# Linear attention brought into the wide attention's block, with its numerators ahead of the projection and its division ahead of the addition

## The chip, the cores and the metric

The kernel runs on one NeuronCore of a Trainium2 chip. The metric is the device time of one execution in microseconds (us); lower is better. The core's engines run separate instruction streams: TensorE (matmuls and transposes; in the profile PE, and PEld for its weight loads), VectorE (DVE), ScalarE (ACT), GpSimd (POOL) and SyncE (SP, which only issues DMAs here). They are ordered against each other by semaphores: an instruction waits until a counter has reached a value, and counts another one up when it is done.

## The reference, cut to what matters

A batch of 16 sequences of 128 tokens with 256 features goes through two decoder layers, each with an attention, a cross step over a context `ctx` and a feed-forward step; every step is added to `x`. The change lies in the second layer, where the wide attention (16 heads of 128) is followed by a linear attention over `ctx` and by a mixture of experts:

```python
q = heads(layernorm(x) @ Wq.T + bq)       # 16 heads of 16
k = heads(ctx @ Wk.T + bk); v = heads(ctx @ Wv.T + bv)
q_prime = relu(q @ Wqf.T)                  # 64 features a head
k_prime = relu(k @ Wkf.T) * mask
kv  = einsum('bhnf,bhne->bhfe', k_prime, v)
num = einsum('bhmf,bhfe->bhme', q_prime, kv)
den = einsum('bhmf,bhf->bhm', q_prime, k_prime.sum(2))
x = x + (num / (den + 1e-8)) @ Wo.T + bo
```

## The kernel before, in words

`kernel` runs two stages. The first holds all of layer one and the wide attention. The second, `stage_linear_attention_and_expert_mix` (L2480), holds linear attention and the expert mixture. Between them every engine drains, the block ends with a barrier of all engines, GpSimd clears the semaphores and a second barrier follows (`release_semaphores`, L59 to L63).

**Products.** `product` (L39) multiplies two float32 matrices, each split into a rounded high part and a rest, by three matmuls of type fp32r: high by high, high by low, low by high (L41, L42, L43). Operands for it are split by a copy on ScalarE and a subtraction on VectorE. A plain float32 matmul shows as two TensorE records.

**Wide attention, last group.** Its four groups of four sequences each run 16 heads (`group`). Per head t, TensorE does the scores of the next head (L1072), the q and k projections of the one after, the output projection of the former head, the transposes of the probabilities (L1113), values for a later head, and the weighing of values (`weigh`, L1123). VectorE masks, takes the row maximum, copies k (L1488) and the transposed probabilities (L1536), and makes the low part of the weighed values (L1549) after ScalarE has made the high one (L1330). In the last group the heads 14 and 15 have no projections ahead of them. After head 15, VectorE adds four banks to `x` (L1561).

**Linear attention** (`linear_attention`) works by batches (sequences) n = 0 to 15, four to a quarter g; j is the place in the quarter. Its prologue, before the loop: load `ctx` for the first quarter and then for the rest, load five small tensors, split the four weights into high and low, normalise x of the second quarter, and on TensorE three products to fill the time (L1898), queries and keys of quarter 0, query features (L1801), key features (L1812), values, and `key_values(0)`.

The loop, in TensorE's order, for each n: `key_features(n+1)` (L1812), `project(n-1)` (in the last batch after the next one), `numerators_and_denominators(n)` (L1835), then, by j, query features of the next quarter (L1801, j = 2, 3), queries (j = 1, 2) and keys (j = 0, 1; for quarter 1 also n = 2), transposes of the normalised x (L164), `values(n+2)`, and `key_values(n+1)` (L1822). From n = 12 on, transposes for the expert mixture take the place of those of the next quarter.

`key_values` makes kv for two heads at once: 8 matmuls with 128 columns of `kp` as weights and 64 columns of `va` moving. Of the four blocks of each product only the two of one head with itself are used. `numerators_and_denominators` has 16 matmuls, each with 32 columns of weights, on the four strips of 32 columns of the array in turn. `project` reads `oT`, the high and low part of the output of the division.

ScalarE, for each n: the denominators plus 1e-8 (`den`, L1974), query features, queries and keys, the high part of the divided output (`keep_o`, L1979), and kv into SBUF (L1968). It also makes the high part of ctx for the next quarter (L1945).

VectorE, for each n: key features with relu and mask (L2044), `update(n-1)`, that is adding the projection to x (L2063), `divide(n)`, a reciprocal (L2050) and a multiplication (L2052), values (L2038), the low part of the divided output (`o_rest`, L2057), low parts of x and of ctx (L175, L2030), and statistics of x (L112 to L119) or its normalisation (L152). At n = 3 it also sets up the expert mixture (L2237 to L2244).

Waits that bind the loop: `key_values(n+1)` writes the bank that `project(n-1)` wrote, so it waits until `update(n-1)` has read it; `numerators_and_denominators(n+1)` waits until `divide(n)` has read its bank; both use kv from ScalarE.

Of the kernel before, what the change touches and what calls it, by code (L numbers as in the profile page):

```python
# [11 lines left out]
P = 128  # L12
# [10 lines left out]

class Chain:


    def __init__(self, eng, sem, it, per):
        self.eng, self.sem, self.it, self.per, self.n = eng, sem, it, per, 0

    def done(self, ins):  # L30
        self.n += 1
        ins.then_inc(self.sem, 1)
        self.eng.wait_ge(self.sem, self.it * self.per + self.n)
# [16 lines left out]
class Program:  # L50
    def __init__(self, nc, io):
        self.nc, self.io = nc, io
        self.sems = []

# [137 lines left out]
def lora_attention(pr, ctx):  # L192
# [55 lines left out]
    lora_loaded = sem("lora_loaded")  # L248
    NLOAD = 6

# [543 lines left out]
def stage_attention_conv_experts_and_wide_attention(pr, lora):  # L794
# [10 lines left out]
    with ExitStack() as ctx:  # L805
        sb = lambda n, shape, dt=F32: ctx.enter_context(nc.sbuf_tensor(f"wa_{n}", shape, dt))
# [33 lines left out]
        w_in = [sem(f"weights_loaded{n}") for n in range(4 * H // VH)]  # L840
# [13 lines left out]
        u_ps, u_ok = sem("lora_in_psum"), sem("lora_added")  # L854
        block = ctx.enter_context(nc.Block())
# [47 lines left out]
        def _(sp):  # L903
            lora_sync(sp)

            def load_piece(hb, m):
                sp.dma_start(pr.wide_raw[hb][:, m], io["wide_w"][hb, :, m]).then_inc(w_in[PIECES.index((hb, m))], 16)
# [15 lines left out]
            sp.dma_start(pr.h_or_w[:], io["li_w"]).then_inc(pr.w_loaded, 16)  # L923

        @block.gpsimd
        def _(pool):
# [14 lines left out]
            def group(it, last):  # L941
                for t in range(H):
# [4 lines left out]
                    if in_range(t + 1, last):  # L947
                        normalise(it * H + t + 1, (t + 1) % 2)

# [15 lines left out]
            for it in range(NG):  # L965
                group(it, it == NG - 1)

        @block.tensor
        def _(pe):
# [169 lines left out]
            def group(it, last):  # L1139
                n_v = G  # L1140
                for t in range(H):
# [22 lines left out]
                    if t == T_TURN:  # L1164
# [3 lines left out]
                        norm.tensor_transpose(pe, next_norm(it))  # L1168
                    weigh(it, t)
                    for unit in late:  # L1170
# [68 lines left out]
            for it in range(NG):  # L1239
                group(it, it == NG - 1)  # L1240

        @block.scalar
        def _(act):
# [17 lines left out]
            def high_part(n):  # L1261
                hb, m = PIECES[n]
                act.wait_ge(w_in[n], 16)
# [49 lines left out]
            def group(it, last):  # L1313
                for t in range(H):
# [69 lines left out]
            for it in range(NG):  # L1384
                group(it, it == NG - 1)

        @block.vector
        def _(dve):
# [135 lines left out]
            def group(it, last):  # L1524
# [3 lines left out]
                for t in range(H):  # L1528
# [26 lines left out]
                    if it == 0 and 1 <= t <= len(PIECES) - FRONT_PIECES:  # L1555
                        low_part(FRONT_PIECES + t - 1)
                    if t == H - 1 and not last:
# [69 lines left out]
            for it in range(NG):  # L1627
                group(it, it == NG - 1)


def first_layer_and_wide_attention(pr):
# [3 lines left out]
    with ExitStack() as ctx:  # L1635
# [29 lines left out]
        stage_attention_conv_experts_and_wide_attention(pr, lora)  # L1665


def linear_attention(pr, ctx, mix):

    nc, io, x, banks = pr.nc, pr.io, pr.x, pr.banks
# [948 lines left out]
```

## Time and profile before

| | |
|---|---|
| time, median of 3 runs | 1010.68 us (1008.8 to 1012.94) |
| the profiled execution's own time | 1011.92 us |
| its span, first to last instruction | 1010.1 us |
| TensorE busy | 959.6 us, 95% of the span |
| VectorE busy | 636.9 us, 63% |
| ScalarE busy | 482.0 us, 48% |
| GpSimd busy | 239.3 us, 24% |
| mean granted TensorE clock | 0.98 of full speed |

Busy time says how much of the span an engine had an instruction in work. The granted clock is a share of 2.4 GHz; the rows show either 1.0 or 0.5 of it (1.2 GHz). The chain of waits is followed back from the last instruction, each step to what released it; a chain row gives its start, its length, and the engine, tile and line. A timeline row gives the start, the length, the engine, the line and the operation, and in brackets how long the engine idled before it and what ended that.

### The profile page before, as it was taken

The numbers are of one execution on the slowest core, as the hardware profiler recorded it, in microseconds if no ns is written. First come the engines' busy times: TensorE is split into PE (matmuls) and PEld (weight loads), VectorE is DVE, ScalarE is ACT, GpSimd is POOL, SyncE is SP. The second block draws the span as 40 slices with busy tenths as digits, with TensorE's granted clock in tenths as the row PEclk, the third lists the DMA queues.
The fourth block names the chain that finished last, engine by engine and source line by source line (L and its number), as shares of the span: only waits on it lengthen the run. The fifth ranks groups of instructions, "written<-read, shape, count | busy, mean of one in ns | idle before, by whom it ended". The sixth has DMA issues, their size and how long they took to land. (4 is left out here: it accounts for less than half of the span.)

```text
span 1010.1 us, 19622 instructions
## 1 busy us (share of the span) xinstructions
PE 959.6 (95%) x7403; PEld 820.1 (81%) x7403; DVE 636.9 (63%) x1399; ACT 482.0 (48%) x1611; POOL 239.3 (24%) x257
## 2 busy tenths in 40 slices
PE   7999999999999999999999999999999888999877
PEld 5777777898788888888888888888888757777757
DVE  5678887897765666544554645464554555777854
ACT  3887877334455454353434534444444343344421
POOL 3455786760011111111111111111111130110000
PEclk9999999999999999999999999999999997899979
DMA  8000000003400000000000000000000070000002
GB/s 303 27 2 2 2 2 1 2 15 133 177 14 1 1 1 1 2 1 1 1 1 1 1 1 16 28 1 1 1 2 1 1 268 1 2 1 2 2 1 84
DMA packets 10395, 27.85 MB, mean 28 GB/s; under 512 B 1792, under 2 KB 6944, under 8 KB 9664
## 3 DMA queue, kind: packets, MB, share of 16 engines
q1 hardware_dynamic: 9584, 26.41, 7.2%
q8 instruction: 60, 0.98, 0.4%
q10 hardware_dynamic: 720, 0.20, 0.1%
q14 instruction: 31, 0.25, 0.1%
HBM read 24.51 MB, written 2.10 MB: 26 GB/s over the span
## 5 line engine op out<-in xcount | busy, mean ns | idle before, releaser
L938 POOL TENSOR_TENSOR wa_prob<-wa_prob,wa_rsum 128x512 f32<-128x512 f32 x64 | 67.5, 1055 | 412.5 <-DVE wa_rsum L1493 412.5
L1296 ACT ACTIVATE wa_prob<-wa_prob,wa_negmax 128x128 f32<-128x128 f32 x256 | 99.8, 391 | 56.8 <-DVE wa_negmax L1482 56.6
L41 PE MATMUL bank<-norm_xT_hi,wide_hi 128*128 128x512 f32 x256 | 106.0, 414 | 0.2 <-DVE norm_xT_lo L175 0.2
L42 PE MATMUL bank<-norm_xT_lo,wide_hi 128*128 128x512 f32 x256 | 101.0, 395 | 0.0
L43 PE MATMUL bank<-norm_xT_hi,wide_lo 128*128 128x512 f32 x256 | 101.0, 395 | 0.0
L1549 DVE TENSOR_TENSOR wa_z_lo<-bank,wa_z_hi 128x512 fp32r<-128x512 f32 x64 | 44.3, 691 | 86.6 <-ACT wa_z_hi L1330 86.2
L562 ACT ACTIVATE v_prob<-bank,la_negmax 128x128 f32<-128x128 f32 x256 | 91.1, 399 | 1.1 <-DVE la_negmax L640 1.1
L1304 ACT COPY wa_q<-bank 128x512 f32<-128x512 f32 x64 | 37.5, 586 | 99.0 <-PE bank L43 99.0
L1311 ACT COPY wa_v<-bank 128x512 f32<-128x512 f32 x64 | 37.3, 585 | 97.1 <-PE bank L43 97.1
L308 POOL TENSOR_TENSOR v_prob<-v_prob,la_rsum 128x512 f32<-128x512 f32 x64 | 66.5, 1041 | 52.5 <-DVE la_rsum L645 52.4
L41 PE MATMUL bank<-wide_hi,wa_z_hi 128*128 128x256 f32 x256 | 73.6, 287 | 1.7 <-DVE wa_z_lo L1549 1.4
L159 POOL TENSOR_TENSOR norm_rstd<-norm_rstd,minus_half 128x4 f32<-128x4 f32 x23 | 24.8, 1079 | 205.4 <-DVE norm_rstd L119 174.4
L1123 PEld LDWEIGHTS bank<-wa_probT,wa_v 128*128 128x128 f32 x512 | 65.4, 191 | 9.7 <-DVE wa_probT L1536 4.0
L1488 DVE COPY wa_k<-bank 128x512 f32<-128x512 f32 x64 | 44.3, 692 | 45.2 <-PE bank L43 44.9
L43 PE MATMUL bank<-wide_hi,wa_z_lo 128*128 128x256 f32 x256 | 72.4, 283 | 0.0
L42 PE MATMUL bank<-wide_lo,wa_z_hi 128*128 128x256 f32 x256 | 72.3, 282 | 0.0
L1123 PE MATMUL bank<-wa_probT,wa_v 128*128 128x128 f32 x512 | 68.2, 276 | 1.9 <-DVE wa_probT L1536 1.9
L1536 DVE COPY wa_probT<-bank 128x512 f32<-128x512 f32 x64 | 44.0, 688 | 40.7 <-PE bank L1113 40.7
L1072 PE MATMUL bank<-wa_k,wa_q 128*128 128x128 f32 x512 | 67.6, 275 | 0.0
L1072 PEld LDWEIGHTS bank<-wa_k,wa_q 128*128 128x128 f32 x512 | 62.7, 192 | 0.4
L562 ACT ACTIVATION_READ_ACCUMULATOR v_prob<-bank,la_negmax 128x1 f32 x256 | 61.0, 238 | 0.0
L43 PEld LDWEIGHTS bank<-norm_xT_hi,wide_lo 128*128 128x128 f32 x256 | 48.0, 187 | 11.8
(282 smaller groups left out, 2462.8 us busy)
## 6 DMA issues: line engine op xcount, KB each, us to landing
wide_raw<-in_wide_w SPq DMA_DIRECT2D x16, 512.0 KB, 6.4
em_w<-in_em_w SPq DMA_DIRECT2D x1, 4096.0 KB, 16.1
x<-in_x SPq DMA_DIRECT2D x4, 512.0 KB, 4.8
lc_kt<-in_ctx_rev SPq DMA_DIRECT2D x1, 2048.0 KB, 10.6
lc_toep<-in_toeplitz SPq DMA_DIRECT2D x1, 2048.0 KB, 14.5
out_x<-x SPq DMA_DIRECT2D x8, 256.0 KB, 2.9
li_kt<-in_ctx_rev SPq DMA_DIRECT2D x1, 1536.0 KB, 8.2
w_or_y<-in_l_w SPq DMA_DIRECT2D x1, 1024.0 KB, 6.5
```

The source lines that it names most:

```text
L41: nc.tensor.matmul(out, a[0], b[0], start=start, stop=False, skip_group_check=True)
L42: nc.tensor.matmul(out, a[0], b[1], start=False, stop=False, skip_group_check=True)
L43: return nc.tensor.matmul(out, a[1], b[0], start=False, stop=stop, skip_group_check=True)
L308: nc.gpsimd.tensor_tensor(own, own, rsum[:, n % NS, :].unsqueeze(2).to_broadcast([P, 4, P]), ALU.mult)\
L562: last = nc.scalar.activation(prob[:, n % NP, s, :], b_s[n % RG][:, s * P:(s + 1) * P], ACT.Exp, bias=negmax[:, n % NS, s:s + 1], accum_ou ...
L938: nc.gpsimd.tensor_tensor(prob[:, s], prob[:, s], rsum[:, s, :].unsqueeze(2).to_broadcast([P, G, P]), ALU.mult).then_inc(prob_ok, 1)
L1072: last = nc.tensor.matmul(b_s[s][:, t], q[:, s, t], k[:, s, t], start=True, stop=True)
L1123: last = nc.tensor.matmul(b_z[:, j * P:(j + 1) * P], v[:, g % 2, j, m * HD:(m + 1) * HD], probT[:, h_ % 2, j, :], start=True, stop=True)
L1296: last = nc.scalar.activation(prob[:, s, j, :], prob[:, s, j, :], ACT.Exp, bias=negmax[:, s, j:j + 1], scale=SCALE, accum_out=sums[:, s, j ...
L1488: nc.vector.tensor_copy(k[:, s, :], b_p[1][:, :]).then_inc(k_ok, 1)
L1536: nc.vector.tensor_copy(probT[:, t % 2], b_t[:, :].rearrange("p (j k) -> p j k", j=G))\
L1549: nc.vector.tensor_tensor(z[1][:, t % 2, :], b_z[:, :], z[0][:, t % 2, :].bitcast(F32), ALU.subtract).then_inc(z_lo, 1)
```

## The change

The two stages become one, `both_layers`. The barrier pair and the clearing of semaphores between them go; the events of linear attention and of the mixture reuse semaphores of layer one that nothing waits on any more, each with a base (`Event`, `reached`). The buffers of linear attention lie where those of the layer one attention and convolution and the first half of the wide weights were.

The prologue moves into the last group of the wide attention, at fixed heads t. The products that filled time go. Loads of ctx are issued when head 3 is projected. The split of ctx is done once for all four quarters, ahead of the loop. `project` becomes a plain float32 product. `key_values` becomes 16 matmuls of 64 columns of weights and 32 moving columns, two heads of a pair on the two halves of the array's columns. On TensorE `numerators_and_denominators(n)` goes ahead of `project(n-1)`; on VectorE `divide(n)` ahead of `update(n-1)`. The set-up of the mixture moves to n = 1 and n = 5, and the transposes of its similarity matrix from behind the loop into n = 14. The high part of a wide weight now waits for all four loads of its quarter.

```diff
+Event = namedtuple("Event", "sem base")
+def reached(eng, event, count):
+    eng.wait_ge(event.sem, event.base + count)
...
-            sp.dma_start(pr.wide_raw[hb][:, m], io["wide_w"][hb, :, m]).then_inc(w_in[PIECES.index((hb, m))], 16)
+            sp.dma_start(pr.wide_raw[hb][:, m], io["wide_w"][hb, :, m]).then_inc(w_in[hb], 16)
...
-            act.wait_ge(w_in[n], 16)
+            act.wait_ge(w_in[hb], 16 * 4)
...
+                    if last and t == H - 1:
+                        linear.tensor_keys(pe, 0)
                     weigh(it, t)
+                    if last:
+                        linear.tensor_early(pe, t)
+                        norm.enter_stage(2, 1, b_p)
+                    if last and t == H - 1:
+                        linear.tensor_keys(pe, 1)
...
+                    if last:
+                        linear.scalar_early(act, t)        # after z_hi
...
+                    if last:
+                        linear.vector_early(dve, t)        # after z_lo and low_part
```

In `linear_attention`:

```diff
+    KT_AT, W_AT = 6, 10
+    QUERIES_AT, KEYS_AT = 14, 15
+    STATS_AT, CLEAR_AT, APPLY_AT = 7, 10, 14
...
+    def tensor_early(pe, t):
+        if t == QUERIES_AT:
+            pe.wait_ge(norm.s_lo, DC * norm.split(0))
+            reached(pe, w_lo, 3)
+            for m in range(DC):
+                queries(pe, 0, m, banks[m])
+    def tensor_keys(pe, m):
+        reached(pe, qT_ok, m + 1)
+        keys(pe, 0, m, banks[m])
...
+    def scalar_early(act, t):
+        if KT_AT <= t < KT_AT + NG:
+            reached(act, kt_in, 16 * NG)
+            nc.scalar.copy(kt[0][:, :, own], kt32[:, :, own]).then_inc(kt_hi.sem, 1)
+        if W_AT <= t < W_AT + 3:
+            nc.scalar.copy(w[0][:, n], w32[:, n]).then_inc(w_hi.sem, 1)
+        if t == QUERIES_AT:
+            for m in range(DC):
+                keep_qT(act, 0, m, banks[m])
+        if t == KEYS_AT:
+            for m in range(DC):
+                keep_kT(act, 0, m, banks[m])
+    def vector_early(dve, t):
+        if KT_AT <= t < KT_AT + NG:
+            nc.vector.tensor_tensor(kt[1][:, :, own], kt32[:, :, own], kt[0][:, :, own].bitcast(F32), ALU.subtract)
+        if W_AT <= t < W_AT + 3:
+            nc.vector.tensor_tensor(w[1][:, n], w32[:, n], w[0][:, n].bitcast(F32), ALU.subtract)
+        if t in (STATS_AT, APPLY_AT):
+            if t == STATS_AT:
+                norm.vector_stats(dve, 1)
+            else:
+                norm.vector_apply(dve, 1)
...
             for t in range(T):
-                last = nc.tensor.matmul(b_kv[:, t * 2 * VW:(t + 1) * 2 * VW], kp[:, n % 2, t, :],
-                                        va[:, n % 2, 2 * t:2 * t + 2, :], start=True, stop=True)
+                for e in range(2):
+                    last = nc.tensor.matmul(b_kv[F * e:F * e + F, t * VW:(t + 1) * VW],
+                                            kp[:, n % 2, t, F * e:F * e + F], va[:, n % 2, 2 * t + e, :],
+                                            start=True, stop=True)
...
         def project(n):
-            pe.wait_ge(ot_lo, n + 1)
+            reached(pe, o_ok, n + 1)
...
-                last = product(nc, b_kv[:, 0:D], pair(oT, slice(None), n % 2, c), pair(w, slice(None), O, c),
-                               c == 0, c == DC - 1)
+                last = nc.tensor.matmul(b_kv[:, 0:D], o[:, n % 2, c, :], w32[:, O, c, :], start=(c == 0),
+                                        stop=(c == DC - 1))
...
         reached(pe, loaded, 16 * NLOAD)
         query_features(0, 0)
+        first_query_features()          # waits for kT_ok and for the wide attention's last x
         key_features(0)
+        reached(pe, qf_first, 1)
         values(0)
+        turn_x(1, 0)
         key_values(0)
         values(1)
         for n in range(NB):
...
-            if 0 < n < NB - 1:
-                project(n - 1)
             numerators_and_denominators(n)
-            if n == NB - 1:
+            if n > 0:
                 project(n - 1)
...
-            keep_o(n)
...
+            divide(n, chain)
             if n > 0:
                 update(n - 1)
-            divide(n, chain)
...
-            o_rest(n)
...
-            if t + 1 < NG and j == 3:
-                kt_rest(t + 1)
-            if n == 3:
+            if n == SETUP_AT:
                 mix.vector_setup(dve)
+            if n == LENGTH_AT:
+                mix.vector_length(dve)
```

## Rows read from the trace of the kernel before

**Rows 1.** Windows: stretch, its length, busy time (instructions) of each engine, PEclk, DMA.
```profile
836.80:847.00 10.20, 10.20 (x77) 8.76 (x76) 3.84 (x5) 1.79 (x4) 0.00 (x0) 0.51 0.00 0
877.40:884.20 6.80, 6.80 (x64) 5.66 (x64) 4.11 (x8) 1.99 (x5) 0.00 (x0) 0.50 0.00 0
```

**Rows 2.** Chain of waits in the loop: start, length, what.
```profile
837.08 3.31 PE bank L1822 x16
859.91 1.73 PE bank L1822 x16
...
902.85 1.73 PE bank L1822 x16
...
905.46 0.36 PE bank L41
905.82 0.12 PE bank L42
...
907.85 0.23 PE bank L42
...
910.45 1.73 PE bank L1822 x16
927.02 1.73 PE bank L1822 x16
933.56 1.73 PE bank L1822 x16
940.61 1.73 PE bank L1822 x16
```

**Rows 3.** Timeline, TensorE in batch 10, at full clock.
```profile
926.85 1.89 PE L1822 MATMUL bank<-li_va,li_kp 128*128 128x64 f32 x16
928.68 0.73 PE L1812 MATMUL bank<-li_wf,li_kT 32*128 32x128 f32 x16
930.51 1.08 PE L1835 MATMUL bank<-li_qp,li_kv 128*32 128x128 f32 x32
```

**Rows 4.** Timeline, the loop's last batches.
```profile
935.45 1.40 DVE L112 BATCH_NORM_STATS2 norm_stats<-x 128x6 f32<-128x256 f32 x4
937.38 1.28 DVE L2044 TENSOR_SCALAR li_kp<-bank,li_mask 128x1024 f32<-128x1024 f32 x1
...
952.31 0.47 ACT L1974 ACTIVATE li_den<-bank,li_tiny 128x256 f32<-128x256 f32 x1 [0.97 <-PE bank L1835]
952.81 1.97 PE L1822 MATMUL bank<-li_va,li_kp 128*128 128x64 f32 x16 [0.57 <-DVE x L2063]
952.82 1.75 DVE L2050 RECIPROCAL li_rden<-li_den 128x256 f32<-128x256 f32 x1 [0.15 <-ACT li_den L1974]
955.37 0.74 ACT L1968 COPY li_kv<-bank 64x256 f32<-64x256 f32 x2
959.71 0.42 DVE L2063 TENSOR_TENSOR x<-bank,x 128x256 f32<-128x256 f32 x1 [2.16 <-PE bank L43]
964.96 0.42 DVE L2063 TENSOR_TENSOR x<-bank,x 128x256 f32<-128x256 f32 x1 [0.92 <-PE bank L43]
```

**Rows 5.** Timeline, TensorE around the stage boundary.
```profile
800.15 1.16 PE L1123 MATMUL bank<-wa_probT,wa_v 128*128 128x128 f32 x8 [0.43 <-DVE wa_probT L1536]
806.94 0.39 PE L41 MATMUL bank<-wide_hi,wa_z_hi 128*128 128x256 f32 x1 [1.40 <-DVE wa_z_lo L1549]
811.62 0.67 PE L1898 MATMUL bank<-h_or_w 128*128 128x512 f32 x1 [2.99 <-PEq L62]
```

**Rows 6.** Timeline, VectorE in the last group's head 8, and one low part of ctx.
```profile
755.19 0.69 DVE L1488 COPY wa_k<-bank 128x512 f32<-128x512 f32 x1 [0.86 <-PE bank L43]
757.06 0.69 DVE L1536 COPY wa_probT<-bank 128x512 f32<-128x512 f32 x1 [1.18 <-PE bank L1113]
...
869.11 1.22 DVE L2030 TENSOR_TENSOR li_kt_lo<-li_kt,li_kt_hi 128x1024 fp32r<-128x1024 f32 x1
```

**Rows 7.** Timeline, plain float32 products with 256 moving columns.
```profile
259.70 1.96 PE L1006 MATMUL bank<-le_u,xe 128*128 128x256 f32 x8
```

More of the change, by code:

```diff
@@ L1 @@
+from collections import namedtuple
 from contextlib import ExitStack
@@ L248, in lora_attention @@
     lora_loaded = sem("lora_loaded")
+    pr.finished += [Event(q_ps, DC * NG), Event(q_ok, DC * NG), Event(k_ps, DC * NG), Event(k_ok, DC * NG),
+                    Event(v_ps, 2 * NG), Event(v_ok, 2 * NG), Event(s_ps, N), Event(max_ok, N), Event(exp_ok, N),
+                    Event(r_ok, N), Event(prob_ok, N), Event(t_ps, N), Event(t_ok, N), Event(av_ps, N),
+                    Event(ot_hi, NB), Event(ot_lo, NB), Event(o_ps, NB), Event(x_ok, NB), Event(xb_ok, NB),
+                    Event(kk_first, 4 * CONV_C), Event(c_ps, CONV_H), Event(c_ok, CONV_H), Event(w_ps, 4),
+                    Event(w_f32, 4), Event(w_hi, 4), Event(w_lo, 4), Event(bias_ps, 1), Event(bias_ok, 1),
+                    Event(qb_ok, 1), Event(v_zero, 1), Event(loaded, 16 * 6), Event(lora_loaded, 16 * 2)]
     NLOAD = 6
@@ L805, in stage_attention_conv_experts_and_wide_attention @@
     with ExitStack() as ctx:
-        sb = lambda n, shape, dt=F32: ctx.enter_context(nc.sbuf_tensor(f"wa_{n}", shape, dt))
+        sb = lambda n, shape, dt=F32: layer.enter_context(nc.sbuf_tensor(f"wa_{n}", shape, dt))
         sem = lambda n: pr.sem(f"wa_{n}")
@@ L839, in stage_attention_conv_experts_and_wide_attention @@
         loaded = sem("masks_loaded")
-        w_in = [sem(f"weights_loaded{n}") for n in range(4 * H // VH)]
+        w_in = [sem(f"weights_loaded{n}") for n in range(H // VH)]
         w_hi, w_ok = sem("weights_hi"), sem("weights_ready")
@@ L854, in stage_attention_conv_experts_and_wide_attention @@
         u_ps, u_ok = sem("lora_in_psum"), sem("lora_added")
+        pr.wide_o_ps, pr.wide_u_ps, pr.wide_x_ok = o_ps, u_ps, x_ok
+        pr.finished += [Event(kk_ok, 4), Event(sq_ok, 2), Event(c_ps, 3 * CH), Event(c_ok, 3 * CH),
+                        Event(yq_ok, NG * C), Event(slot_ps, NG * C), Event(cx_ok, NG * G), Event(new_ps, G),
+                        Event(nbias_ok, 1)]
+        layer.close()
+        mix = ExpertMix(pr)
+        linear = linear_attention(pr, lambda n, shape, dt=F32: ctx.enter_context(nc.sbuf_tensor(n, shape, dt)), mix)
+        mix.allocate(ctx)
         block = ctx.enter_context(nc.Block())
@@ L1556, in group @@
                         low_part(FRONT_PIECES + t - 1)
+                    if last:
+                        linear.vector_early(dve, t)
                     if t == H - 1 and not last:
```

1494 lines of the change are left out of this document (747 added, 747 removed).

## The prediction

> **What bounds the kernel now.** The profile was read in this order: the page, the chain of waits from its end backwards, windows over the stages, and the timeline on both sides of the stage boundary. Three stretches matter.
>
> The first is the boundary. `weigh` of head 14 ends at 800.15 + 1.16 = 801.3. The last projection starts at 806.9 after 1.40 us of waiting for the low part, x is then added, and the second stage's first product starts at 811.6, after 2.99 us in which TensorE waited for the barrier [rows 5]. From there to `key_values(1)` at 837.1 [rows 2] comes the prologue, where TensorE waits for splits, copies and the loaded context. So 801.3 to 837.1 is 35.8 us.
>
> The second is the loop. At full clock its chain is TensorE's own work: the starts of `key_values` are 7.6 us apart for j = 0 (902.85 to 910.45), 16.6 for j = 1 and 2 together, 6.5 for j = 3 and 7.05 from n = 12 on [rows 2]. Two stretches, 10.2 and 6.8 us long, ran at a granted clock of 0.51 and 0.50, that is 1.2 GHz [rows 1]; in both every TensorE instruction takes about twice as long (3.31 for 1.73 us) [rows 2].
>
> The third is the loop's end: `key_values(15)` at 952.8, the last reciprocal only behind the addition at 959.7, the last addition at 965.0 [rows 4]: 12.2 us. Behind it nothing on the path is changed.
>
> **Part A, boundary and prologue.** After the change, TensorE's work from 801.3 on is: queries of quarter 0, 12 passes of 512 columns at 0.23 [rows 2] and a start, 3.0; four transposes, half of the eight passes of `weigh`, 0.5; projection of head 14, 12 passes at 0.12 [rows 2], 1.5; first half of the keys 1.45; `weigh` of head 15 0.95; second half of the keys 1.45, which covers the wait for z that was 1.40 [rows 5] all but 0.25; projection of head 15, 1.65. Sum 10.7, so 812.0. The products that filled time, the barrier, the weights' split and the context's load (issued around head 4, used from head 6) are off the path.
>
> Then the path alternates. Query features 1.1, behind which VectorE makes the last four additions to x, 1.5 together; the second half of the query features 1.1; VectorE's two copies and key features, 1.4 + 1.3 [rows 4], with 0.4 of gaps, 3.1; then `key_values(0)` 1.1, values 0.9, key features 0.85 [rows 3], numerators 1.15 [rows 3], values 0.9, transposes 0.5. Sum 11.1: `key_values(1)` at 823.1.
>
> What the last group pays: ScalarE's and VectorE's new work sits behind the low part of z. A low part of ctx takes 1.22; VectorE waits 0.86 and 1.18 in every such head [rows 6], so it is covered. At head 7 statistics of x come on top, 1.40 and small followers [rows 4], some 2.2 in all. Delayed by 1.7 + 2.2, less 2.0 of waits and 0.5 of slack, `weigh` comes 1.4 late. If nothing is hidden the four context splits, three weight splits and the statistics cost up to 10, if all is hidden 0; I take 1.4, since the waits are measured. GpSimd's clears fall into its long waits. So A ends at 824.5: 12.6 us less. Bounds: 17 less to 5 less (prologue at half clock, or the last group's work uncovered).
>
> The later wait for wide weights: all four loads of quarter 1 must land before ScalarE's third split, ahead of a copy that itself waits for TensorE. I price it at 0, bound 2.
>
> **Part B, the loop to `key_values(15)`, 115.7 us before** (837.1 to 952.8).
>
> `key_values` today: 16 passes in 1.89 [rows 3], 0.118 a pass with 128 columns of weights and 64 moving, at full clock. The pass is too long for its 64 moving columns: a pass of 512 columns takes 0.23, one of 256 takes 0.12 [rows 2], so weights set its pace. After: 32 passes with half the columns of weights, on the two column halves in turn. If the halves load side by side, 16 pairs at about 0.06 and 0.15 of fill, 1.1. If they load one after the other, 32 at 0.059 = 1.9, no gain. A third bound, each pass waiting for the one before, is in the rivals. Nearest row: `numerators_and_denominators`, 32 passes on four column strips in turn, takes 1.08, 0.034 a pass, though each has 128 columns moving, as much as others pay 0.11 for alone [rows 3]. Strips do work side by side there. I take 1.1: 0.8 less a batch.
>
> A rule speaks against this. Those 0.034 us do not show whether the loads overlapped as well, as 32 columns load in about a quarter of the time of 128 [rows 3]. The Trainium skill, "TensorE: Matmul & The Clock Gate", Part 3, says that a weight load runs beside matmuls in flight only where the row group differs; all these passes use all rows. "TensorEngine Tiling (Array Packing)", Key Properties, says that different tiles can load and multiply in parallel. By the second the sum stands; by the first it is that of the second rival below.
>
> `project`: six passes 0.36 + 5 x 0.12 = 0.96 [rows 2] become two plain float32 products, four passes. Eight such take 1.96 [rows 7], 0.22 a pass, so 0.9 + 0.15: 0.1 more a batch. The ScalarE and VectorE steps between division and projection go; they are off the path except at the end.
>
> Order: together a batch has 0.7 less on TensorE. But now `key_values(n+1)` waits for `update(n-1)`, which stands behind `divide(n)`, which waits for the numerators of n. That closes a ring: `key_values` 1.1, key features 0.9, numerators 1.1 and a switch 0.15, denominators 0.5, reciprocal 1.8, multiplication 0.4, addition 0.45 (durations of rows 3 and 4 with hand-overs) = 6.4. Nothing can go below 6.5 a batch. `kv`'s copy, 0.74 [rows 4], is covered by key features, 0.73 [rows 3], to about 0.1.
>
> Sum: n = 1 and 2: 16.6 and one more half of keys, 2.1, is 18.7, less 1.4 is 17.3. n = 3: 6.5. Two quarters: 7.6 - 0.7 = 6.9, 16.6 - 1.4 = 15.2, 6.5, so 28.6 each. n = 12, 13, 14: 6.5 each, 19.5. Total 100.5, 15.2 less. Of that 9 is half clock and VectorE waits in the first quarters (the same template with today's prices gives 106.9), 6 is work. The waits go because ctx is split ahead and the mixture's set-up is spread out. Bounds: 19 less (ring at 6.2) to 4 less (kv no faster, 3 us at half clock back, VectorE late at j = 1).
>
> **Part C, the end, 12.2 before.** `key_values(15)` 1.15, kv copy 0.85, numerators 1.2, denominators 0.6, reciprocal 1.8, multiplication 0.45, projection 1.1, addition 0.45, that is 7.6, and 0.5 for a clock that may drop there: 8.1. 4.1 less; bounds 5 and 2. The reciprocal no longer stands behind the addition at 959.7, and the split of the output is gone.
>
> Sum: 12.6 + 15.2 + 4.1 = 31.9 less. The profiled execution's own time, 1011.9, becomes 980.0; the median of the runs is 1.2 lower, so 979.
>
> **Rivals.**
> 1. *The wait moves to VectorE.* Its stages in a batch, with statistics or a normalisation, delay the ring to about 7.2 a batch, and the prologue keeps 3 us at half clock. For: its steps in the ring (reciprocal, key features, addition) fill most of a batch already [rows 4]. Against: the low parts of ctx, 1.22 a quarter [rows 6], and the output's split leave it. 14 x 0.5 + 2 = 9 more: 988.
> 2. *Column halves don't load side by side.* 0.8 x 15 = 12 more: 991.
> 3. *It doesn't hide what it moves.* The queries' and keys' passes and delays there only move; the boundary gives 6 less than said: 985.
> 4. *Slower.* The 32 short passes of `key_values` serialise with the full latency of a record (a record of it is shown longer than its share of the pace) instead of being pipelined. It decides from the point where `key_values` takes 1.1 + 32/16 = 3.1 us a batch, that is 0.1 a pass, since TensorE is the path and all 16 batches pay. At 0.2 a pass, 6.4 a batch, it is 5.3 x 16 = 85 - 32 = 53 slower: 1063. Against: the strips of `numerators_and_denominators` are pipelined.
>
> **Numbers.** Forecast 0.56, rival 1 0.16, rival 2 0.14, rival 3 0.10, rival 4 0.04. The range 970 to 992 takes in the forecast's own bounds and rivals 1 to 3. A measurement of this kernel tells about 0.5%, 5 us, from no change. Faster 0.95, within 0.5% 0.01, slower 0.04.
>
> **What would show it.** In the new profile: no idle of TensorE over 2 us between the last `weigh` and the loop; `key_values(1)` some 12 us earlier; 32 records of `key_values` in about 1.1 us; starts of it 6.5 to 8 us apart, with a wait for VectorE's addition before it where j = 3 and from n = 12 on; the last reciprocal right behind the denominators. Wrong if `key_values` takes 1.9 or more, if TensorE's waits in the last group's heads 6 to 12 exceed 3 us, or if the clock falls for long between the two parts.

## The result, and the profile after

The changed kernel takes 977.98 us (median of 4 runs, 977.52 to 978.13); in the same session the kernel before took 1011.71 us (1008.8 to 1012.94). The ratio is 0.967, 95% interval 0.9647 to 0.9693. The forecast was 979 for the median and 980.0 for the profiled execution, whose own time is 978.1 us.

The first lines of the page after:

```profile
span 976.3 us, 19976 instructions
...
PE 935.4 (96%) x7621; PEld 796.0 (82%) x7621; DVE 628.1 (64%) x1383; ACT 475.7 (49%) x1593; POOL 239.0 (24%) x257
```

The span is 33.8 us shorter. Cut where the prediction cut it, by the starts and ends in the timelines of both kernels (that of before has `key_values(1)` at 836.87, its chain, which the prediction used, at 837.08; the prediction's 12.2 for C ends at the start of the last addition, 965.0, the 12.6 here at its end):

| stretch | before | after | change | forecast |
|---|---|---|---|---|
| A, up to the start of `key_values(1)` | 836.87 | 823.06 | -13.8 | -12.6 |
| B, from there to `key_values(15)` | 115.9 | 100.1 | -15.8 | -15.2 |
| C, from there to the end of the last addition | 12.6 | 9.4 | -3.1 | -4.1 |
| from there to the end of the span | 44.7 | 43.7 | -1.0 | 0 |

TensorE in the timeline after, from `weigh` of head 14 to `key_values(1)` (start, length, engine, line, operation; in brackets the idle time before it and what ended it). It answers to [rows 5]:

```profile
800.89 1.16 PE L2033 MATMUL bank<-wa_probT,wa_v 128*128 128x128 f32 x8 [0.43 <-DVE wa_probT L2459]
...
807.95 1.05 PE L2033 MATMUL bank<-wa_probT,wa_v 128*128 128x128 f32 x8
...
810.40 0.39 PE L50 MATMUL bank<-wide_hi,wa_z_hi 128*128 128x256 f32 x1
...
812.02 1.14 PE L987 MATMUL bank<-li_qT,li_wf 32*128 32x512 f32 x8
813.69 1.14 PE L995 MATMUL bank<-li_qT,li_wf 32*128 32x512 f32 x8 [0.53 <-DVE x L2486]
815.44 0.73 PE L1006 MATMUL bank<-li_wf,li_kT 32*128 32x128 f32 x16 [0.61 <-ACT li_qp L1161]
...
818.08 1.13 PE L1017 MATMUL bank<-li_va,li_kp 128*64 128x32 f32 x32 [0.43 <-DVE li_va L1250]
...
823.06 1.13 PE L1017 MATMUL bank<-li_va,li_kp 128*64 128x32 f32 x32
```

The last projection (810.40) has no wait in front of it; 1.40 us stood there before. The longest idle time in the prologue is 0.61 us, where the barrier alone cost 2.99.

The chain of waits after, its `key_values` pieces (start, length, what; the loop's other pieces left out). They answer to [rows 2]:

```profile
823.13 1.08 PE bank L1017 x32
...
882.52 1.08 PE bank L1017 x32
...
890.39 1.08 PE bank L1017 x32
...
897.82 1.08 PE bank L1017 x32
...
904.05 1.14 PE bank L1017 x32
...
916.84 1.08 PE bank L1017 x32
...
923.19 1.14 PE bank L1017 x32
```

From start to start: 7.87 and 7.43 us for j = 1 and 2, 6.3 to 6.4 from n = 11 on. The whole of B by the starts in the timeline is 7.88, 9.53, 6.46, then 6.89, 7.87, 7.41, 6.46, then 6.89, 7.87, 7.43, 6.30, and 6.36, 6.36, 6.42.

TensorE in one batch after, at full clock, which answers to [rows 3] and holds the new projection:

```profile
890.32 1.12 PE L1017 MATMUL bank<-li_va,li_kp 128*64 128x32 f32 x32
891.38 0.73 PE L1006 MATMUL bank<-li_wf,li_kT 32*128 32x128 f32 x16
892.29 1.08 PE L1031 MATMUL bank<-li_qp,li_kv 128*32 128x128 f32 x32 [0.19 <-ACT li_kv L1175]
893.30 1.13 PE L1041 MATMUL bank<-h_or_w,li_o 128*128 128x256 f32 x4
```

The 32 passes of `key_values` take 1.12 us where 16 took 1.89. The granted clock in windows after (stretch, length, busy time and instructions of PE, PEld, DVE, ACT, POOL, then PEclk and the DMA share):

```profile
812.00:832.00 20.00, 18.10 (x274) 13.82 (x274) 16.11 (x31) 8.23 (x17) 0.25 (x1) 1.00 0.53 214
837.00:923.00 86.00, 79.89 (x1212) 61.54 (x1210) 66.07 (x123) 39.23 (x106) 9.64 (x12) 1.00 0.01 2
925.20:928.60 3.40, 3.40 (x36) 2.71 (x37) 0.97 (x1) 0.47 (x1) 0.00 (x0) 0.50 0.00 0
```

In the prologue and in the loop the clock stays at 1.00, 2.4 GHz: both stretches of [rows 1] are gone. So is a third one, in the prologue of the kernel before, which the prediction does not name. And part C of the kernel before ran partly at 1.2 GHz as well. Its windows there:

```profile
811.50:822.00 10.50, 10.38 (x35) 5.93 (x36) 7.47 (x20) 5.49 (x11) 5.29 (x7) 0.84 0.77 236
952.50:965.00 12.50, 8.15 (x68) 6.79 (x68) 8.18 (x19) 4.38 (x22) 0.85 (x1) 0.77 0.00 1
```

As the rows know only the two levels, 0.84 and 0.77 mean about 3.4 us of 10.5 and 5.7 us of 12.5 at 1.2 GHz. After the change the clock first falls behind the one long wait of the loop, for 3.4 us. The timeline after of the loop's end shows that wait, and answers to [rows 4]:

```profile
920.40 1.75 DVE L1262 RECIPROCAL li_rden<-li_den 128x256 f32<-128x256 f32 x1
...
922.62 0.42 DVE L1269 TENSOR_TENSOR x<-bank,x 128x256 f32<-128x256 f32 x1
...
923.19 1.13 PE L1017 MATMUL bank<-li_va,li_kp 128*64 128x32 f32 x32 [2.07 <-DVE x L1269]
...
925.15 1.92 PE L1031 MATMUL bank<-li_qp,li_kv 128*32 128x128 f32 x32 [0.83 <-ACT li_kv L1175]
...
927.13 0.47 ACT L1181 ACTIVATE li_den<-bank,li_tiny 128x256 f32<-128x256 f32 x1 [2.03 <-PE bank L1031]
927.63 1.75 DVE L1262 RECIPROCAL li_rden<-li_den 128x256 f32<-128x256 f32 x1 [2.85 <-ACT li_den L1181]
...
930.58 0.66 PE L178 MATMUL bank<-ident,norm_xn 128*128 128x128 f32 x4 [1.23 <-ACT em_xT L1590]
...
931.08 1.03 PE L1041 MATMUL bank<-h_or_w,li_o 128*128 128x256 f32 x4
...
932.21 0.42 DVE L1269 TENSOR_TENSOR x<-bank,x 128x256 f32<-128x256 f32 x1 [1.02 <-PE bank L1041]
```

Two things are to be seen. `key_values(15)` waited 2.07 us for the addition of batch 13, which stood behind the division of batch 14: the ring of the new order. And the last reciprocal is indeed right behind its denominators, but the output that it gives, ready at 929.8, is taken up only at 931.08: ahead of the projection TensorE had transposes for the expert mixture in its queue, and waited 1.23 us for ScalarE's copies of earlier ones.

What the last group paid, in VectorE's timeline after (it answers to [rows 6]):

```profile
751.99 0.69 DVE L2472 TENSOR_TENSOR wa_z_lo<-bank,wa_z_hi 128x512 fp32r<-128x512 f32 x1 [2.13 <-ACT wa_z_hi L2249]
752.94 1.22 DVE L1223 TENSOR_TENSOR li_kt_lo<-li_kt,li_kt_hi 128x1024 fp32r<-128x1024 f32 x1 [0.26 <-ACT li_kt_hi L1141]
754.08 1.40 DVE L126 BATCH_NORM_STATS2 norm_stats<-x 128x6 f32<-128x256 f32 x4
...
760.69 0.69 DVE L2472 TENSOR_TENSOR wa_z_lo<-bank,wa_z_hi 128x512 fp32r<-128x512 f32 x1 [1.17 <-ACT wa_z_hi L2249]
```

The first row belongs to head 7, the last to head 8. The low part of z of head 8 comes 8.70 us after that of head 7; up to head 11 every other step takes 7.84 to 7.86, with or without a split of ctx or a weight, and the steps to heads 12, 13 and 14 take what they took before within 0.01 (6.46, 7.33 and 4.68). So the statistics of head 7 cost 0.85 and the other new work of VectorE up to there nothing.

### The profile page after: what moved, and what is told of

The parts are those of the page before. It is cut to its first block, busy times and chain, and to the rows that moved or that the text cites. A ratio compares the mean times of both kernels' runs of the same rounds, so it can differ in the third digit from the quotient of the medians.

```text
span 976.3 us, 19976 instructions
## 1 busy us (share of the span) xinstructions
PE 935.4 (96%) x7621; PEld 796.0 (82%) x7621; DVE 628.1 (64%) x1383; ACT 475.7 (49%) x1593; POOL 239.0 (24%) x257
## 4 chain that ended last, share of the span: by engine, by line
PE 83%; DVE 8%; ACT 5%; issue 3%; DMA 0%; POOL 0%; SPq 0%; DVEq 0%; ACTq 0%; POOLq 0%
PE bank L50 15%; PE bank L52 14%; PE bank L51 14%; PE bank L2033 6%; PE bank L1982 5%; PE bank L392 3%; PE bank L402 3%; PE bank L2023 3%; PE bank L1897 2%; PE bank L1906 2%; PE bank L1031 2%; PE bank L414 2%; PE bank L178 2%; PE bank L1041 2%; PE bank L1017 2%
## 5 line engine op out<-in xcount | busy, mean ns | idle before, releaser
L50 PE MATMUL bank<-norm_xT_hi,wide_hi 128*128 128x512 f32 x256 | 106.0, 414 | 0.2 <-DVE norm_xT_lo L189 0.2
L2223 ACT COPY wa_q<-bank 128x512 f32<-128x512 f32 x64 | 37.6, 587 | 93.6 <-PE bank L52 93.6
L2033 PEld LDWEIGHTS bank<-wa_probT,wa_v 128*128 128x128 f32 x512 | 65.4, 191 | 10.7 <-DVE wa_probT L2459 5.0
```

The lines of the kernel that those rows point to most:

```text
L50: nc.tensor.matmul(out, a[0], b[0], start=start, stop=False, skip_group_check=True)
L2033: last = nc.tensor.matmul(b_z[:, j * P:(j + 1) * P], v[:, g % 2, j, m * HD:(m + 1) * HD], probT[:, h_ % 2, j, :], start=True, stop=True)
```

## The experiments

Eleven kernels ran, in three sessions. The kernel before, run beside them, took 1011.49, 1010.99 and 1010.62 us (medians of 7, 9 and 7 runs). Starts within the span differ by up to 2.3 us from kernel to kernel for reasons that lie ahead of the last group (the low part of z of head 7 comes at 750.29 in e6 and at 752.58 in e1), so steps are compared from start to start.

### Is the gain of the loop the passes of `key_values`?

**e1_kv_wide**: the changed kernel with the former `key_values`, 128 columns of weights and 64 moving.

```diff
-                for e in range(2):
-                    last = nc.tensor.matmul(b_kv[F * e:F * e + F, t * VW:(t + 1) * VW],
-                                            kp[:, n % 2, t, F * e:F * e + F], va[:, n % 2, 2 * t + e, :],
+                last = nc.tensor.matmul(b_kv[:, t * 2 * VW:(t + 1) * 2 * VW], kp[:, n % 2, t, :],
+                                        va[:, n % 2, 2 * t:2 * t + 2, :], start=True, stop=True)
```

> The changed kernel with key_values in its old form: 8 matmuls with 128 columns of weights and 64 moving. Theory (the new form gains because the two column halves load and multiply side by side, and all 15 batches of the loop pay TensorE's time): key_values takes 1.9 us again instead of 1.1, 0.75 to 0.8 more in each of 15 batches, less where VectorE's ring is the longer one: 10 to 12 us slower than the changed kernel, so about 989. Rival (the ring through VectorE sets the pace already, and the short form is hidden): under 4 us slower.

**e2_halves_apart**: the changed kernel, the same 32 passes in another order: first all on one half of the array's columns, then all on the other.

```diff
-            for t in range(T):
-                for e in range(2):
+            for e in range(2):
+                for t in range(T):
```

> The changed kernel with the same 16 matmuls of key_values, but the eight of the first column half all ahead of the eight of the second, so that neighbours no longer use different halves. Theory (the gain is that neighbouring passes on different halves run side by side): key_values takes about 32 x 0.056 = 1.8 us instead of 1.1, 10 us slower than the changed kernel, about 988. Rival (a pass with half the columns of weights costs a third of one with all, whatever stands beside it): 1.1 us, no difference.

Measured: 990.54 us (ratio 0.9796, 0.9781 to 0.9811) and 990.41 us (0.9799, 0.9783 to 0.9816). One row of `key_values` from the timeline of e1, and one from that of e2:

```profile
897.53 1.89 PE L1016 MATMUL bank<-li_va,li_kp 128*128 128x64 f32 x16
```

```profile
895.88 1.84 PE L1017 MATMUL bank<-li_va,li_kp 128*64 128x32 f32 x32
```

With the same instructions in another order the gain is gone: 1.85 us against 1.12. So halving the columns brings nothing by itself (two passes of 0.058 us do the work of one of 0.118); what brings it is that two neighbouring passes lie on different halves. That is the forecast's first case, and the second rival fell. In the loop, e1 needs 110.0 us from `key_values(1)` to `key_values(15)` and the changed kernel 100.1: the halves are worth 9.8 us there, 12.6 in the whole. Of the rest most lies behind `key_values(15)`: from its start to the end of the last addition e1 takes 12.2 us and the changed kernel 9.4, of which the longer `key_values` is 0.8; e1 runs at 1.2 GHz from 936.2 to 946.4 there. Both kernels came out some 2 us slower than expected (expected 989 and 988).

**e4_before_kv_halves**: the kernel before, with the new `key_values` alone.

```diff
-                last = nc.tensor.matmul(b_kv[:, t * 2 * VW:(t + 1) * 2 * VW], kp[:, n % 2, t, :],
-                                        va[:, n % 2, 2 * t:2 * t + 2, :], start=True, stop=True)
+                for e in range(2):
+                    last = nc.tensor.matmul(b_kv[F * e:F * e + F, t * VW:(t + 1) * VW],
+                                            kp[:, n % 2, t, F * e:F * e + F], va[:, n % 2, 2 * t + e, :],
+                                            start=True, stop=True)
```

> The kernel before with the new form of key_values alone. Theory (TensorE's path): 0.78 less in 16 batches, 12 less, of which VectorE's waits in the first quarters take some back: 8 to 12 us faster than before, about 1001. Rival (the loop is bound by VectorE's waits): under 4 faster.

Measured: 1000.11 us (0.9895, 0.988 to 0.991), `key_values` 1.13. So the edit pays in either kernel, 11.4 us here and 12.6 there; the gain does not need the rest of the change.

### What are the two new orders worth?

**e3_old_orders**: the changed kernel with both orders undone. **e10_old_pe_order** undoes that of TensorE alone, **e9_old_dve_order** that of VectorE alone.

```diff
# e3 and e10, TensorE
+            if 0 < n < NB - 1:
+                project(n - 1)
             numerators_and_denominators(n)
-            if n > 0:
+            if n == NB - 1:
                 project(n - 1)
# e3 and e9, VectorE
-            divide(n, chain)
             if n > 0:
                 update(n - 1)
+            divide(n, chain)
```

> The changed kernel with both old orders: project(n-1) ahead of numerators_and_denominators(n) on TensorE (but for the last batch), update(n-1) ahead of divide(n) on VectorE. Theory (the loop is TensorE's own work at full clock, so order costs or gives little there; the last batch gains 1.5 us from the division not waiting behind the addition): within 3 us of the changed kernel, 1 to 3 slower. Rival A (the new orders carry the loop's gain, as the division starts earlier): 6 to 15 us slower. Rival B (the new orders cost, as key_values waits for the addition behind the division): 2 to 5 us faster than the changed kernel.

> The changed kernel with TensorE's old order alone: project(n-1) ahead of the numerators of n (but in the last batch); on VectorE the division stays ahead of the addition. Theory: the ring through the division gets the projection as one more member, 1.0 to 1.1 us on top of 6.4, so 7.3 to 7.5 us a batch; key_values starts 12 batches of 6.4 to 6.9 us now become 7.3 or more, those of 7.4 and 7.9 hardly change: 6 to 9 us slower than the changed kernel, 984 to 987 us. So either new order is worth nothing without the other. Rival: TensorE's own work hides it, 977 to 979 us.

> The changed kernel with VectorE's old order alone: update(n-1) ahead of divide(n); on TensorE the numerators stay ahead of the projection. It tells which of the two new orders costs 2.07 us in front of key_values(15). Theory: that wait is the ring key_values, numerators, division, update; with the update ahead of the division the ring is open, so key_values(15) follows key_values(14) by 4.4 to 4.8 us instead of 6.41; the starts for n = 12 to 14 stay at 6.3 to 6.4 apart because TensorE's work sets them; the last division then comes up to 1.5 us later and gives part back. 975.5 to 977 us. Rival: with the update ahead, divide(n) waits for project(n-1) in every batch and the numerators of n+1 wait for the division, 0.2 to 0.5 us in each of 14 batches: 980 to 985 us.

Measured: e3 976.69 us (0.9662, 0.9645 to 0.968), e10 988.12 (0.9786, 0.9751 to 0.9822), e9 975.62 (0.966, 0.9628 to 0.9693). The timeline of e10, `key_values` behind the ring and the projection within it:

```profile
909.06 1.12 PE L1017 MATMUL bank<-li_va,li_kp 128*64 128x32 f32 x32 [1.29 <-DVE x L1271]
...
911.06 1.10 PE L1041 MATMUL bank<-h_or_w,li_o 128*128 128x256 f32 x4 [0.22 <-issue]
...
931.32 1.13 PE L1017 MATMUL bank<-li_va,li_kp 128*64 128x32 f32 x32 [3.14 <-DVE x L1271]
```

a window of e10 behind that last wait:

```profile
932.70:953.20 20.50, 14.81 (x70) 9.47 (x71) 10.56 (x39) 4.67 (x22) 2.06 (x3) 0.50 0.00 1
```

and the timeline of e9, `key_values(15)`:

```profile
921.37 1.13 PE L1017 MATMUL bank<-li_va,li_kp 128*64 128x32 f32 x32 [0.44 <-DVE x L1269]
```

In e10 seven of the fourteen distances between `key_values` are 7.37 to 7.40 us, in batches that have 6.3, 6.4, 6.5 or 6.9 in the changed kernel: a ring shows by one period whatever the batch holds. Less the projection, some 1.0 us, that is 6.35, an estimate for the ring of the changed kernel. A stretch of 20.5 us at 1.2 GHz follows the wait of 3.14, and e10 ends 1 us above what was expected. In e9 the ring is open; the distance to `key_values(15)` falls from 6.42 to 4.79 us, and the rest stay within 0.02 but for n = 11 and 12 (6.01 and 6.50 for 6.30 and 6.36). So up to n = 13 it is TensorE's queue, and not the ring, that sets the pace of the changed kernel; in batches 12 and 13 the queue also holds 0.5 us of waiting for ScalarE. The ring's period and the short batches, 6.35 and 6.3 to 6.5 us, lie side by side by chance. VectorE's new order needs TensorE's; with it, it is no better than the old pair, and e3 and e9 are at or below the changed kernel.

The two new orders are not alike, though. Measured from the low part of z of head 7 to the end of the span, the changed kernel takes 224.3 us, e3 223.5, e9 221.6 and e10 234.8. From `key_values(1)` to `key_values(14)` e3, with the projection ahead, takes 95.1 us, and e9, with the numerators ahead, 93.6. So in the traces TensorE's new order alone gains about 1.9 us over the old pair, and VectorE's on top of it costs 2.7, most of it in front of `key_values(15)` and by the clock behind it. The intervals of e3 and e9 overlap that of the changed kernel, so these differences of 1 to 3 us are read from the traces, not from the times. For e3 the expectation (1 to 3 us slower) had the wrong sign; neither of its rivals came in the time.

### What does the join bring?

**e5_pe_late**: the changed kernel; TensorE alone makes quarter 0's queries and keys behind the last projection. **e6_all_late**: all engines do the early work only there; the loads of ctx stay early.

```diff
# e5
-                    if last and t == H - 1:
-                        linear.tensor_keys(pe, 0)
                     weigh(it, t)
-                    if last:
-                        linear.tensor_early(pe, t)
-                        norm.enter_stage(2, 1, b_p)
-                    if last and t == H - 1:
-                        linear.tensor_keys(pe, 1)
...
+            linear.tensor_early(pe, 15)        # QUERIES_AT = 15
+            linear.tensor_keys(pe, 0)
+            linear.tensor_keys(pe, 1)
# e6: the same, and likewise on each other engine, behind its last head
+            for t in range(H):
+                linear.vector_early(dve, t)    # scalar_early, gpsimd_early
```

> The changed kernel, but TensorE makes the queries and keys of quarter 0 only behind the projection of head 15 instead of around the two last weighings; all other engines keep their early work. Theory: those passes fill TensorE's waits for the low part of z (1.40 us in the kernel before) and for the projection's hand-overs, and the copies of queries and keys are ready when asked for, so moving them back costs about 3 us: key_values(1) at 826 instead of 823.1, 981 us. Rival (rival 3 of the prediction: it only moves work and hides nothing): key_values(1) stays at 823 to 824, 978 us.

> The changed kernel without any barrier, but every engine starts the work of the linear attention's prologue (splits of ctx and of three weights, statistics, queries and keys) only behind its own work for head 15; the loads of ctx stay early. It tells the missing barrier from the overlap. Theory: the low parts of ctx and weights (4 x 1.2 and 3 x 0.6 us on VectorE, statistics 1.4 and normalisation) then lie on the path in front of the queries, so key_values(1) comes 8 to 12 us later than 823.1, at 831 to 835, and the whole takes 986 to 990 us; the head-7 stall of 0.85 us goes. Rival: the barrier and the fill products were the whole cost and the order within the block is indifferent: key_values(1) at 823 to 825, 978 to 980 us.

Measured: e5 980.94 us (0.97, 0.9687 to 0.9713), e6 991.59 (0.9813, 0.9791 to 0.9835). The timeline of e5 has the waits that the early passes filled, and that of e6 the splits on the path:

```profile
807.72 0.39 PE L50 MATMUL bank<-wide_hi,wa_z_hi 128*128 128x256 f32 x1 [1.40 <-DVE wa_z_lo L2468]
...
818.31 0.73 PE L1006 MATMUL bank<-li_wf,li_kT 32*128 32x128 f32 x16 [1.42 <-ACT li_qp L1161]
```

```profile
816.69 0.77 PE L50 MATMUL bank<-norm_xT_hi,li_w_hi 128*128 128x512 f32 x1 [9.88 <-DVE li_w_lo L1228]
```

A window of e6 behind the beginning of that idle time:

```profile
810.70:820.90 10.20, 4.21 (x10) 3.37 (x11) 7.06 (x19) 0.69 (x1) 6.66 (x9) 0.50 0.84 361
```

Measured from the low part of z of head 7, `key_values(1)` comes after 71.1 us in the changed kernel, 74.1 in e5, 85.0 in e6 and 84.8 in the kernel before. The early products of TensorE are worth 3.0, the whole overlap 13.9, as much as part A in all (13.8). Without the overlap the join gains nothing here, though it has no barrier and no filling products: TensorE waits for the splits instead, part of it at 1.2 GHz. (e6 splits ctx for all four quarters there, the kernel before for one, so it does not price the barrier by itself.) The third rival fell. The expectation for e5 was met; that for e6 had `key_values(1)` at 831 to 835, where it came at 835.3, and the time 1.6 us too low.

### Why did the kernel before stall in the first quarters?

**e7_setup_early**: the kernel before, the mixture's set-up at n = 1.

```diff
-            if n == 3:
+            if n == 1:
                 mix.vector_setup(dve)
```

> The kernel before, only the set-up of the expert mixture on VectorE moved from n = 3 to n = 1. Theory: the set-up at n = 3, beside low parts of ctx, makes TensorE wait in n = 3 and 4 and thereby brings the half-clock stretch at 877.4 to 884.2; without it key_values(5) comes 4 to 7 us earlier and the kernel takes 1005 to 1007 us. Rival: the wait comes from the low part of ctx and the statistics, whatever the set-up does: 1010 to 1012 us, with a half-clock stretch in the same place.

Measured: 1004.7 us (0.9936, 0.9922 to 0.9949). The timeline of the kernel before, around batch 4:

```profile
871.69 2.79 POOL L1756 TENSOR_TENSOR x<-x,li_out_bias 128x256 f32<-128x256 f32 x4
871.75 2.88 DVE L2244 TENSOR_SCALAR em_simT<-em_simT,em_sim_len 32x256 f32<-32x256 f32 x1 [0.20 <-POOL em_sim_len L2219]
874.56 1.26 DVE L2044 TENSOR_SCALAR li_kp<-bank,li_mask 128x1024 f32<-128x1024 f32 x1
...
876.30 1.96 PE L1822 MATMUL bank<-li_va,li_kp 128*128 128x64 f32 x13 [1.79 <-DVE x L2063]
```

and the window of e7 that answers to the second of [rows 1]:

```profile
877.40:884.20 6.80, 6.73 (x68) 5.66 (x68) 5.53 (x15) 2.26 (x4) 0.00 (x0) 1.00 0.01 2
```

`key_values(5)` comes at 874.1 instead of 876.3, the clock stays at 1.00, and `key_values(9)` at 905.3 instead of 910.3. So 1.8 us of waiting, given back as 2.2, cost 2.9 more by the clock that fell behind it. Another 1.9 us are gained behind `key_values(15)`, where nothing was edited and the trace of e7 has 3.4 us less at 1.2 GHz. The expectation had `key_values(5)` 4 to 7 us earlier; it came 2.2 earlier, and the rest of the gain goes with the clock. One small edit takes a fifth of what the whole change does.

### A version that beats both

**e8_mixed**: the changed kernel, the old orders in batch 14 alone, and the statistics of x at head 5, which has no split of ctx. **e11_dve_stats**: VectorE's old order throughout, and the same statistics.

```diff
-    STATS_AT, CLEAR_AT, APPLY_AT = 7, 10, 14
+    STATS_AT, CLEAR_AT, APPLY_AT = 5, 10, 14
# e8 only
+            if n == NB - 2:
+                project(n - 1)
             numerators_and_denominators(n)
-            if n > 0:
+            if n > 0 and n != NB - 2:
                 project(n - 1)
...
+            if n == NB - 2:
+                update(n - 1)
             divide(n, chain)
-            if n > 0:
+            if n > 0 and n != NB - 2:
                 update(n - 1)
```

> The changed kernel with two edits: in batch 14 alone the old orders (project(13) ahead of the numerators of 14, update(13) ahead of divide(14)), and the statistics for x of the second quarter at head 5 of the last group instead of head 7. Theory: the ring through the division, 2.07 us of waiting in front of key_values(15), goes in the one batch where it decides, so key_values(15) comes 1.5 to 1.8 us earlier (about 921.4) while the other batches keep their 0.1 to 0.2; and the stall of 0.85 us in head 7 goes, as head 5 has no split of ctx. Together 2 to 3 us: 975.5 us. Rival: the statistics stall head 5 as much, and what is gained in batch 14 is lost in half clock at the end: 977.5 to 978.5 us.

> The changed kernel with VectorE's old order alone and the statistics of x at head 5 instead of head 7. Theory: 0.86 us from head 7 (as the kernel that mixed the orders showed) and up to 2 us in front of key_values(15), less what the last division gives back: 974.5 to 976 us, no better than the kernel with the old orders in batch 14 alone (973.8). Rival: the late division costs more than it gives: 977 to 978 us.

Measured: e8 973.83 us (5 runs, 972.56 to 975.21; ratio 0.9632, 0.9618 to 0.9646), e11 974.35 (0.9654, 0.9618 to 0.9689). The timeline of e8, `key_values(15)` and the last addition:

```profile
919.66 1.13 PE L1017 MATMUL bank<-li_va,li_kp 128*64 128x32 f32 x32
...
927.98 0.42 DVE L1271 TENSOR_TENSOR x<-bank,x 128x256 f32<-128x256 f32 x1 [0.34 <-PE bank L1041]
```

The low part of z of head 8 is 7.84 behind that of head 7 again (8.70), the wait of 2.07 before `key_values(15)` is gone (4.29 from start to start instead of 6.42), and behind it 8.7 us remain to the end of the last addition instead of 9.4, as the clock stays up. That is 0.9 + 2.1 + 0.7 = 3.7 of the 4.3 by which the span is shorter; the other 0.6 lies ahead of the last group. e8 is 1.7 us faster than expected, as it gained 2.1 and not 1.5 to 1.8 in front of `key_values(15)` and kept the clock behind it. The whole interval lies below that of the changed kernel, if barely. e8 is 0.5 us ahead of e11, which is no difference that these runs can tell.

## Why the prediction was right, point by point

The places of the gain were right in all three parts, and so were the causes, but for that of the short batches (part B). That the median came within 1 us is partly luck. The span fell by 33.8 us where the sum had 31.9: A and B gave 1.2 and 0.6 more than said, C 1.0 less, and the stretch behind it, priced at 0, gave 1.0. Then 1.2 us were taken off for the distance between the profiled execution and the median; in the changed kernel that distance is 0.15.

**Part A** (-13.8; said -12.6). The stall of the last group came at head 7 from the statistics, as said, but it is 0.85 us instead of 1.4: the new work delays VectorE's mask of the next head by 3.4 us (752.72 before, 0.61 behind the start of z's low part; 756.01 after, 4.02 behind it), not by the 3.9 of the sum, and the 2.5 of waits and slack take the rest. The 3.4 us at 1.2 GHz in the prologue of the kernel before were not in the sum. TensorE's work up to the first features took 9.97 us from the end of `weigh(14)` instead of 10.7. From there to `key_values(1)`, 11.1 was said and 11.04 measured. Four loads for one split of the wide weight, priced at 0, show no wait in the trace either.

**Part B** (-15.8; said -15.2). The pattern of the batches came as forecast: 17.3 said and 17.41 measured for n = 1 and 2; 6.5 and 6.46; twice 28.6, and 28.6 and 28.5; 19.5 and 19.1 for the last three. The parts of it: `key_values` 1.12 (1.1 said), the projection 1.05 to the next start (1.05). By the runs the halves are worth 9.8, and the rest, e1 against the kernel before, 6.0: 9.2 won where that kernel waited or ran at 1.2 GHz in its first quarters (its distances 12.82, 9.56 and 11.45 are 8.55, 7.56 and 8.55 in e1), and 3.2 given back, 1.9 of it in front of `key_values(15)`. The text had 9 for the waits and the clock and 6 for the work, which is 9.8 less 3.2, or 6.6. Its 106.9, the loop at full clock by prices of before, does not follow from its rows: they give 107.8 with 7.05 for each of the last three batches, or 106.0 with the 5.3 that the last one took; so its split is good to 1 us.

That two column halves load side by side was the open point. The row of 1.12 us and e2's 1.85 decide it. The Trainium skill, "TensorEngine Tiling (Array Packing)", Key Properties, says that different tiles can load and multiply in parallel, and the trace agrees: a pair of passes on the two halves takes 0.07 us, less than two of e2's 0.058. The Trainium skill, "TensorE: Matmul & The Clock Gate", Part 3, lets a weight load overlap with matmuls in flight only where the row group differs; read strictly, all passes here would take e2's time, and they do not. The 0.11 us that the prediction gives for 128 moving columns alone stands in none of its rows: [rows 3] has 0.118 for 64 moving columns behind 128 columns of weights. It served only to say that strips work side by side; the sum's 1.1 does not use it.

The ring was named and sized rightly (6.4; e10 gives 6.35 less its projection), but the reason given for the short batches was not: the prediction let the ring set their 6.5 us and looked for a wait for the addition where j = 3 and from n = 12 on. The trace has 0.22 us of it before `key_values(12)`, 2.07 before `key_values(15)` and none in the others, and in e9, where the ring is open, the batches of 6.46 and 6.36 stay. The number was right because TensorE's queue happens to be as long as the ring. Nor was the ring's price weighed against leaving the orders alone. In the template the last batch, n = 14, got 6.5 like the others, and that it could be 4.3 (e8) was not seen, though the kernel before had 5.31 there. The two orders together, which give the change its name, gain nothing: e3 without them is as fast.

**Part C** (-3.1; said -4.1). On the same ends, 12.6 and 8.1, the sum said -4.5. Its 12.2 was also not a price at full clock, as about 5.7 us of it ran at 1.2 GHz. The terms from `key_values(15)` to the multiplication were 7.6 - 1.55 = 6.05 and 0.5 for the clock; measured 6.65. What is missing is 1.2 us between the output of the division, 929.84, and the projection, 931.08: the queue of TensorE ahead of the projection was not read. The 1.0 us behind part C is probably the clock, which was low there for 11.0 us before (up to 976.4) and for 6.8 after. e10, with the same instructions there as the changed kernel, speaks for it (44.5 us behind its last addition with 10.5 us at 1.2 GHz, where the changed kernel has 43.7 with 6.8); no run was made to test it.

**The rivals.** The first (the wait moves to VectorE, 7.2 us a batch) did not occur, but e10 shows how near it was: one operation more in the ring and each short batch takes 7.37 to 7.40. The fourth needed 0.1 us a pass; it is 0.035.

## What to carry to other kernels

Where short passes are paced by their weights, as these float32 passes were, try neighbouring passes on different column parts of the array; halving the columns alone brought nothing here (e2), the order of the passes did. When an order is changed so that a step can start earlier, close the ring on paper and compare its period with the busy engine's own work in every kind of batch: where the work is longer, opening the ring buys nothing, and where it is shorter the ring costs (2.1 us in the shortest batch here). Then undo each half of the change of order by itself: here one half gained and the other lost it again. A join of two stages pays by what it lets run beside other work; place each moved piece in a wait that the trace shows.

## What was not expected of the hardware

- A VectorE multiplication of 32 x 256 by a value per row took 2.88 us beside a GpSimd addition of 2.79 us (rows of the kernel before above). In e7, with GpSimd idle, it took 0.34, and 0.33 in the changed kernel, where a GpSimd operation of 1.04 us began 0.17 us behind its start. Other VectorE operations beside the same addition did not grow (masked key features 1.28 us at 870.95 in the changed kernel, the addition at 871.00 to 873.78). Whether GpSimd lengthened it, or only ended with it, was not tested by itself.
- The price of a wait was more than its length: 1.79 us of TensorE's waiting before 876.30 went together with 6.8 us at 1.2 GHz, and 9.88 us in e6 with 10.2 us. In the changed kernel 2.07 us before 923.19 was followed by 3.4 us; e9, with 0.44 us there, has none of it in that place. But the length of the wait does not tell the price: e1 has the same 2.07 us before `key_values(15)` and then 10.2 us at 1.2 GHz.
- One kernel does not always lose the same to the clock. In the third session the kernel before took 1006.7 to 1008.7 us in three executions with a mean granted clock of 0.985, and 1010.6 to 1012.8 in four with 0.976 to 0.98. Differences of a few us between two single traces can be of this kind.
